# A gated Mamba layer and a ternary feed-forward block on one core: where the statistics of nine tiles are computed, and a new order of the prologue

## The reference, cut to what matters

```python
# x: (4, 512, 512), ctx: (4, 512, 256), all fp32
z   = layernorm(x)                               # (x - mean) / sqrt(var + 1e-5)
u   = silu(conv4(ctx @ in_proj.T) + conv_b)      # (4, 512 channels, 512 steps)
dt_low, Bm, Cm = split(x_proj @ u)               # 16 + 16 + 16 rows
dt  = softplus(dt_low @ dt_proj.T + dt_proj_b)
state = state * exp(dt * A) + (dt * u) * B       # scan over 512 steps, 16 states
y   = (sum_n state * C + D * u) * silu(z)
x1  = x + tanh(g_xattn) * y.T
# feed-forward, rows of 512: three matrices quantised to -1, 0, 1 over mean(|w|)
n   = layernorm(x1);  q = round(127 * rmsnorm(n) / max|rmsnorm(n)|)
h   = silu(q @ w_gate) * (q @ w_up)              # 2048 wide
out = x1 + tanh(g_ffn) * (quantise(rmsnorm(h)) @ w_down)
```

## Time and profile before

| | |
|---|---|
| median of 3 runs | 646.84 us (646.74 to 649.95) |
| the profiled execution's own time | 646.95 us |
| its span, first to last instruction | 644.8 us |
| mean granted TensorE clock | 0.947 |
| start of stage 0, first scan | 75.20 us |
| start of stage 4 | 180.41 us |
| start of stage 15 | 545.01 us |

### The profile page before, as it was taken

The page is one execution under the profiler, slowest core; times in us unless marked ns, Lnnn a source line. Parts: engine busy times, 40 slices in busy tenths (PEclk is TensorE's granted clock), DMA queues, the critical chain, the costliest instruction groups (busy, mean ns, idle before and its releaser), DMA issues. The chain is left out here.

```text
span 644.8 us, 9079 instructions
## 1 busy us (share of the span) xinstructions
PE 505.9 (78%) x2966; PEld 345.2 (54%) x2966; DVE 576.1 (89%) x806; ACT 501.0 (78%) x719; POOL 510.6 (79%) x281
## 2 busy tenths in 40 slices
PE   6998585856757687778767887787787878799997
PEld 2443274745644565556545655565555656564553
DVE  2879999999988999998999999999999999987664
ACT  4889699896976686878688787877786878778784
POOL 2534999999989999999989999999899989931100
PEclk9999869989787889998999899999898999999999
DMA  8993910711830100019301111175111010000001
GB/s 296 400 411 107 376 34 33 262 49 41 338 111 1 33 18 22 13 40 347 115 22 33 34 34 35 33 266 190 34 34 34 33 34 17 1 17 18 16 18 50
DMA packets 29986, 64.47 MB, mean 100 GB/s; under 512 B 3682, under 2 KB 11874, under 8 KB 26867
## 3 DMA queue, kind: packets, MB, share of 16 engines
q1 hardware_dynamic: 29938, 63.89, 27.8%
HBM read 55.75 MB, written 8.13 MB: 99 GB/s over the span
## 5 line engine op out<-in xcount | busy, mean ns | idle before, releaser
L701 POOL TENSOR_TENSOR area_s<-area_s,b_bc 128x1024 f32<-128x1024 f32 x128 | 300.6, 2362 | 22.4 <-DVE u_all L1227 17.7
L428 PE MATMUL pY<-ident,area_s 128*128 128x128 f32 x640 | 107.8, 297 | 83.0 <-DVE area_s L1235 81.8
L428 PEld LDWEIGHTS pY<-ident,area_s 128*128 128x128 f32 x640 | 77.7, 151 | 111.6 <-DVE area_s L1235 76.0
L926 ACT ACTIVATE pA<-dt_all,a_neg 128x512 f32<-128x512 f32 x160 | 107.8, 682 | 23.8 <-DVE area_s L1227 14.5
L1227 DVE TENSOR_TENSOR_SCAN area_s<-pA,area_s 128x512 f32<-128x512 f32 x96 | 114.3, 1204 | 3.7 <-ACT pA L926 3.4
L468 PE MATMUL pG<-wq_gu,area_f 128*128 128x512 fp8e4 x448 | 112.6, 391 | 4.7 <-ACT area_f L878 3.2
L1235 DVE TENSOR_TENSOR area_s<-area_s,pC 128x512 f32<-128x512 f32 x144 | 95.3, 664 | 10.9 <-issue 9.1
L693 POOL TENSOR_TENSOR u_all<-u_all 128x1024 f32<-128x1024 f32 x44 | 103.9, 2361 | 0.0
L422 PE MATMUL pC<-ident,xdT 128*128 128x128 f32 x576 | 94.1, 292 | 1.6 <-DVE xdT L1094 1.3
L422 PEld LDWEIGHTS pC<-ident,xdT 128*128 128x128 f32 x576 | 74.0, 149 | 6.8 <-DVE area_s L1235 4.3
L468 PEld LDWEIGHTS pG<-wq_gu,area_f 128*128 128x128 bf16 x448 | 43.8, 101 | 49.6 <-issue 6.6
(11 more groups left out here) (177 smaller groups left out, 970.4 us busy)
## 6 DMA issues: line engine op xcount, KB each, us to landing
b_bc<-bc_rows SPq DMA_DIRECT2D x16, 1024.0 KB, 7.9
area_s<-x SPq DMA_DIRECT2D x32, 256.0 KB, 2.9
u_all<-bc_rows SPq DMA_DIRECT2D x14, 512.0 KB, 5.7
b_bc<-w_gate SPq DMA_DIRECT2D x1, 4096.0 KB, 14.7
dt_all<-x SPq DMA_DIRECT2D x1, 4096.0 KB, 25.0
area_f<-w_up SPq DMA_DIRECT2D x1, 4096.0 KB, 34.5
area_f<-w_down SPq DMA_DIRECT2D x1, 4096.0 KB, 14.9
out<-area_f SPq DMA_DIRECT2D x16, 256.0 KB, 2.1
```

Source lines behind the costliest of these rows:

```text
L428: mm = pe.matmul(pY[:, k * P:(k + 1) * P], src[:, k * P:(k + 1) * P], ident[:, :], is_transpose=True, start=(first and k == 0), stop=(last ...
L701: gp.tensor_tensor(db[c % NDB], du[s % 2].rearrange("p (a l) -> p a l", a=1).to_broadcast([P, CH, L]), b_bc[:, CH * c:CH * c + CH, :], ALU ...
L926: act.activation(exp_bank(s, n), dt_all[:, s, :], ACT.Exp, scale=a_neg[:, s % NT, n:n + 1]).then_inc(S["s_exp"], 1)
```

## The change

Stages. For the nine tiles t with t % 4 not 0 and t < 12, VectorE's `stats` goes. ScalarE computes the sum of the row (`x_sum`), centres with it (`centre`, now sum - 512 x), and sums the squares (`x_deviation`, followed by a small instruction that writes VE). `xn` has two buffers. In kind B this stands at steps 3 and 4, ahead of `copy_xqT` in ScalarE's order; in kind A at steps 9 and 10, after it. `x_scales` of kind B moves from step 13 to step 11. GpSimd's second `x_rstd` of kind A moves behind `dt_u` and `times_b(s + 1, 0)`. In stages 7, 11 and 15 VectorE does the `residual` instead of GpSimd. On TensorE the last two groups of `hq_transpose` move behind `y_sum(s, 6)` and `c_bcast(s, 7)`.

Prologue. VectorE does the fourth sum of |w_gate| too, GpSimd the four roundings of `w_gate` and, for the last chunk, a clip; VectorE then makes that chunk ternary, behind its statistics of x. Five of the statistics of x come earlier, the last sums are ordered anew, and two waits of ScalarE move from the end of the prologue to its first `z_silu`.

```diff
+def own_stats(t):
+    return t % NT == 0 or t >= UNITS - NT
+def own_residual(s):
+    return s % NT == 2 and s >= NT
+BN_AT = [sum(own_stats(i) for i in range(t)) for t in range(UNITS + 1)]
-        xn = carve(area_f, 4608, D)
+        xn = [carve(area_f, 4608, D), w_xp_sb[:, :, :].rearrange("p k n -> p (k n)")]
...
             def w_total(m):
-                    pe.wait_ge(S["k_abv"], NW - 1 + NW * m)
+                    pe.wait_ge(S["k_abv"], NW + NW * m)
...
             dt_proj(1)
             x_proj(1)
+            w_total(0)
             project(12)
             project(13)
             rows_transpose(1)
-            w_total(0)
...
-                    for r in range(HR):
-                        hq_transpose(t2, r, pG)
+                    hq_transpose(t2, 0, pG)
+                    hq_transpose(t2, 1, pG)
                 y_sum(s, 6)
                 c_bcast(s, 7)
+                if t2 >= 0:
+                    hq_transpose(t2, 2, pG)
+                    hq_transpose(t2, 3, pG)
...
+            def w_round(c):
+                gp.wait_ge(S["k_wm"], 3)
+                gp.tensor_scalar(raw(0, c), raw(0, c), w_inv[:, 0:1], MAGIC, ALU.mult, ALU.add).then_inc(S["k_p1"], 1)
+            def w_clip(c):
+                gp.wait_ge(S["k_p1"], c + 1)
+                gp.tensor_scalar(raw(0, c), raw(0, c), MAGIC + 1.0, MAGIC - 1.0, ALU.min, ALU.max).then_inc(S["k_clip"], 1)
+            conv_sums(0, 10)
+            w_round(0)
+            conv_sums(10, 12)
+            w_round(1)
+            conv_sums(12, 14)
+            w_round(2)
+            conv_sums(14, UNITS)
+            w_round(3)
+            w_clip(3)
...
-            times_b(0, 0)
-            times_b(0, 1)
             gp.wait_ge(S["k_st"], 2 * UNITS)
...
-            times_b(0, 2)
-            times_b(0, 3)
+            for c in range(NDB):
+                times_b(0, c)
...
-                residual(s - 1)
+                if not own_residual(s - 1):
+                    residual(s - 1)
...
             silu(9)
-            act.wait_ge(S["c_g0"], 16)
-            w_abs(0, NW - 1)
             rows_out(1)
+            conv_start(12)
+            conv_start(13)
             silu(10)
             silu(11)
-            conv_start(12)
-            conv_start(13)
-            w_sign(0, 0)
             conv_start(14)
             conv_start(15)
+            w_sign(0, 0)
             rows_out(2)
             silu(12)
             silu(13)
             w_sign(0, 1)
-            w_sign(0, 2)
             silu(14)
             silu(15)
-            w_sign(0, 3)
+            w_sign(0, 2)
...
+            def x_sum(t):
+                act.wait_ge(S["s_x1"], (t // NT) * NT + NT)
+                act.wait_ge(S["f_xn"], t)
+                past(act, S["f_xqp"], t - 1)
+                act.activation(xn[t % 2].rearrange("p (a c) -> p a c", a=NT), tile_x1(t), ACT.Copy, accum_out=col(XSUM)).then_inc(S["f_sum"], 1)
+            def x_deviation(t):
+                act.wait_ge(S["f_xn"], t + 1)
...
+                act.activation(place[:, 0:D], xn[t % 2], ACT.Square, accum_out=col(DEV)).then_inc(S["f_dev"], 1)
+                act.wait_ge(S["f_dev"], t - BN_AT[t] + 1)
+                act.wait_ge(S["f_rr"], t)
+                act.activation(col(VE), col(DEV), ACT.Copy, scale=(1.0 + RMS_EPS) / D, bias=RMS_EPS * LN_EPS * D * D).then_inc(S["f_ve"], 1)
...
                     if n == (2 if t1 % NT else 8):
                         scale_x(t1)
+                    if n == 3 and t1 % NT and (t1 + 1) % NT:
+                        x_sum(t1 + 1)
+                        centre(t1 + 1)
+                    if n == 4 and t1 % NT and (t1 + 1) % NT:
+                        x_deviation(t1 + 1)
                     if n == (4 if t1 % NT else 9):
                         copy_xqT(t1, pG[0][:, :])
...
-                    if n == 10 and (t1 + 1) % NT:
+                    if n == 9 and t1 % NT == 0:
+                        x_sum(t1 + 1)
+                    if n == 10 and t1 % NT == 0:
                         centre(t1 + 1)
+                        x_deviation(t1 + 1)
...
+            def w_ternary(c):
+                dve.wait_ge(S["k_clip"], 1)
+                dve.tensor_scalar(ternary(0, c), raw(0, c), -MAGIC, None, ALU.add, saturate=False).then_inc(S["k_p3"], 1)
...
             w_abs(0, 2)
+            w_abs(0, 3)
+            w_means(0)
             taps(10)
-            w_means(0)
-            w_round(0)
-            w_round(1)
+            for i in range(3):
+                x_stats(i)
             taps(12)
             rows_copy(1)
+            x_stats(3)
+            x_stats(4)
             taps(14)
-            w_round(2)
-            w_round(3)
             rows_copy(2)
-            for i in range(UNITS):
+            for i in range(5, UNITS):
                 x_stats(i)
...
+            w_ternary(3)
             w_abs(1, 0)
...
+                    if n == 3 and own_residual(s - 1):
+                        residual(s - 1)
...
-                    if n == (4 if t1 % NT else 8) and (t1 + 1) % NT:
-                        stats(t1 + 1)
-                    if n == 13 and (t1 + 1) % NT:
+                    if n == (11 if t1 % NT else 13) and (t1 + 1) % NT:
                         x_scales(t1 + 1)
```

More of the change, by code:

```diff
@@ L60 @@
 C_STEP = {2: 3, 3: 4, 6: 7, 7: 11, 10: 12, 11: 13, 14: 15, 15: 16}
-VE, RR, M2, REC1, XS, SS, RH, M3, REC2, FAC, MH = range(11)
+def own_stats(t):
[3 more added lines that the diff above has]
+BN_AT = [sum(own_stats(i) for i in range(t)) for t in range(UNITS + 1)]
+VE, RR, M2, REC1, XS, SS, RH, M3, REC2, FAC, MH, XSUM, DEV = range(13)
 PSS, PMH, SPARE = 20, 24, 28
@@ L368, in rows_transpose @@
                 past(pe, S["k_xdT"], b)
+                past(pe, S["k_wm"], min(b, 1))
                 for t in range(NT):
@@ L461, in xq_transpose @@
                 for k in range(NT):
-                    mm = pe.transpose(bank[:, k * P:(k + 1) * P], xn[:, k * P:(k + 1) * P], ident[:, :])
+                    mm = pe.transpose(bank[:, k * P:(k + 1) * P], xn[t % 2][:, k * P:(k + 1) * P], ident[:, :])
                 mm.then_inc(S["f_xqp"], 1)
@@ L661, in _, with conv_sums @@
             gp.wait_ge(S["k_const"], 9)
-            for i in range(UNITS):
-                gp.wait_ge(S["k_tap"], i + 1)
-                gp.wait_ge(S["k_acc"], 2 * i + 2)
-                gp.tensor_tensor(xc[i % 4][:, 1:L], xc[i % 4][:, 1:L], xb[i % 4][:, 1:L], ALU.add).then_inc(S["k_conv"], 1)
+            def conv_sums(first, last):
+                for i in range(first, last):
+                    gp.wait_ge(S["k_tap"], i + 1)
+                    gp.wait_ge(S["k_acc"], 2 * i + 2)
+                    gp.tensor_tensor(xc[i % 4][:, 1:L], xc[i % 4][:, 1:L], xb[i % 4][:, 1:L], ALU.add).then_inc(S["k_conv"], 1)
+            def w_round(c):
[13 more added lines that the diff above has]
+            w_clip(3)
             def residual(s):
@@ L673, in x_rstd @@
             def x_rstd(t):
[L674 removed]
+                gp.wait_ge(S["f_ve"], t + 1)
                 past(gp, S["f_xs"], 5 * t)
@@ L747, in _ @@
                 times_c(s, 1)
-                if t1 % NT == 0:
-                    x_rstd(t1 + 1)
                 times_b(s, NDB + 3)
@@ L753, in _ @@
                     times_b(s + 1, 0)
+                if t1 % NT == 0:
+                    x_rstd(t1 + 1)
                 times_c(s, 2)
@@ L863, in centre @@
             def centre(t):
-                act.wait_ge(S["f_bn"], 3 * t + 2)
-                past(act, S["f_xqp"], t)
-                act.activation(xn.rearrange("p (a c) -> p a c", a=NT), tile_x1(t), ACT.Identity, scale=-1.0, bias=mv[:, 0:1]).then_inc(S["f_xn"], 1)
+                past(act, S["f_xqp"], t - 1)
+                out = xn[t % 2].rearrange("p (a c) -> p a c", a=NT)
+                if own_stats(t):
+                    act.wait_ge(S["f_bn"], 2 * BN_AT[t] + 2)
+                    act.activation(out, tile_x1(t), ACT.Identity, scale=-1.0, bias=mv[:, 0:1]).then_inc(S["f_xn"], 1)
+                else:
+                    act.wait_ge(S["f_sum"], t - BN_AT[t] + 1)
+                    act.activation(out, tile_x1(t), ACT.Identity, scale=-float(D), bias=col(XSUM)).then_inc(S["f_xn"], 1)
+            def x_sum(t):
+                act.wait_ge(S["s_x1"], (t // NT) * NT + NT)
+                act.wait_ge(S["f_xn"], t)
+                past(act, S["f_xqp"], t - 1)
+                act.activation(xn[t % 2].rearrange("p (a c) -> p a c", a=NT), tile_x1(t), ACT.Copy, accum_out=col(XSUM)).then_inc(S["f_sum"], 1)
+            def x_deviation(t):
+                act.wait_ge(S["f_xn"], t + 1)
+                if (t - 1) % NT:
+                    place = squares_out(t)
+                    past(act, S["f_sq"], 2 * t - 3)
+                else:
+                    place = squares_out(t - 1)
+                    past(act, S["f_dn"], t - 2)
+                act.activation(place[:, 0:D], xn[t % 2], ACT.Square, accum_out=col(DEV)).then_inc(S["f_dev"], 1)
```

(11 more changed lines are left out.)

25 lines of the change are left out of this document (10 added, 15 removed).

## The result

The changed kernel takes 651.69 us (median of 20 runs, 649.82 to 652.55), the kernel before 648.59 us beside it (20 runs, 645.47 to 652.54): ratio 1.0052, 95% interval 1.0037 to 1.0066. My 647.0 was wrong, the time lies 0.2 us above the range, and my chance for "slower" was 0.17. Of the 4.7 us between 647.0 and 651.69, 3.1 are the change, which I had put at 0.2; the rest is the kernel before itself, which measures 1.75 us more in 20 runs than in the three that I started from (646.84). The profiled execution has a span of 649.4 us against 644.8, granted clock 0.942 against 0.947.

A forecast was written before the change was run, and what follows sets the result against it. The prediction took ScalarE's chain around the gate's silu to bound the later half of a stage as much as VectorE. Stages + 1.6 and prologue - 1.4 on 646.95 gave 647.15 us, range 639.5 to 651.5.

The forecast's parts named there:

- kind B: Stages 5, 6, 9, 10, 13, 14: 2.8 us won, 2 x 0.1 at full clock plus 4 x 0.65 at low clock.
- kind A: Stages 4, 8, 12: ScalarE's statistics delay the first silu; 8 and 12 lose 1.45 us each, 4 nothing; 2.9 us lost.
- prologue: Work ahead of the stages: 1.4 us won; bounds 4.0 won and nothing won.
- the residual's price: Stages 7, 11, 15: VectorE's residual costs 0.66 us like another VectorE product, 0.6 less overlap, replacing 1.27 on GpSimd.
- Kind C: Stages 7, 11, 15: residual ahead of h_max and later transposes of h lose 0.5 us each, 1.5 us; upper bound 3 x 1.2.
- the rounding's row: Prologue: VectorE's ternary chunk priced from the trace's rounding at 1.3 to 2.3 us, 1.8 used.
- ScalarE's new work: Per tile, nine times: sum and sum of squares at 0.8 us each plus a small instruction of 0.3, 1.9 us.
- the 0.65 us for each low-clock stage: Stages 5, 9, 13, 14: x_scales lies in the product's wait for TensorE, so 0.65 us won each, between nothing and 1.0.
- ScalarE's standstill: In kind B, ScalarE's wait before copy_xqT, up to 4.1 us, holds the 2.5 us of statistics work at no cost.
- The wait for the store: Prologue: z_silu(1) needs the last store_bc, landing at 81.2 us, so it goes 1.4 us earlier, not 4.
- the third rival: Prologue: GpSimd rounds at its two-input rate, 4.7 us, making z_silu(1) 9.3 us late; 658 us, chance 0.09.
- The first rival: Whole kernel: VectorE is the bound after all, its saved time is kept; 8.0 us won, 639, half 643; chance 0.30.

The follow-up runs named there:

- experiment 2: Changed kernel with TensorE's old order of the transposes of h, residuals still on VectorE: 649.34 us, 1.0017 of the kernel before.
- experiment 5: Kernel before with only the residuals of stages 7, 11 and 15 moved to VectorE at step 3: 652.97 us, 1.0054 of the kernel before.
- experiment 4: Changed kernel with VectorE's residual one step later, where GpSimd is idle: 645.77 us, 0.9955 of the kernel before.
- experiment 1: Changed kernel with the three residuals back on GpSimd, nothing else: 644.27 us, 0.9932 of the kernel before.
- experiment 6: Against experiment 1: statistics of tile t1 + 1 in stages 4, 8 and 12 back on VectorE; 641.66 us, 0.9863 of the kernel before.
- experiment 9: Kernel before with only the new prologue, its stages untouched: 646.19 us, 0.9964 of the kernel before.
- experiment 7: Against experiment 1: x_scales of kind B back at step 13 instead of 11; 636.96 us, 0.9797 of the kernel before.
- experiment 8: Against experiment 1: the prologue's last store_bc issued ahead of three loads in the DMA queue; 644.38 us, 0.9903 of the kernel before.
- the best version: Changed kernel with the edits of experiment 1, experiment 6, experiment 7 and experiment 8 together: 633.97 us, 0.9748 of the kernel before.

## Why the prediction was wrong

**The step that failed is the residual's price.** "Three residuals come, at the 0.66 us of the like product on VectorE" took `gated_y` of the earlier trace rows as the like product. It has the engine, shape and type, but it reads pY from PSUM; the residual reads szT and area_s from SBUF, while GpSimd is busy 31.22 of 31.30 us in stage 11, nearly all of it with products of two SBUF tensors. The true price there was 1.73 to 2.56 us (experiments 2 and 5 and the kernel after), 0.68 where GpSimd was idle (experiment 4). Kind C: +1.5 predicted, +5.8 measured, and undoing it wins 7.4 us, more than the whole 4.7 by which the forecast was off. The bound I gave (3 x 1.2) did not hold it either: it was made of rows of other instructions, none of which met that condition. The trace before could have raised the doubt. It has no row of the residual's kind beside a busy GpSimd, but it shows the two engines holding each other up, in the four roundings of the earlier trace rows:

```profile
43.53 2.47 DVE L1115 TENSOR_SCALAR b_bc<-b_bc,w_inv 128x2048 f32<-128x2048 f32 x2
51.37 4.06 DVE L1115 TENSOR_SCALAR b_bc<-b_bc,w_inv 128x2048 f32<-128x2048 f32 x2
```

```profile
48.05 2.50 POOL L666 TENSOR_TENSOR area_s<-area_s 128x511 f32<-128x511 f32 x2 [7.35 <-DVE area_s L1076]
50.88 3.48 POOL L666 TENSOR_TENSOR area_s<-area_s 128x511 f32<-128x511 f32 x2 [0.32 <-DVE area_s L1076]
```

Two roundings take 2.47 us while GpSimd is idle (1278 ns each in the mean), and the other two 4.06 (2071 ns each) beside GpSimd's convolution sums, which take 3.48 instead of 2.50. The mean of all four, 1675 ns, hid it, and my "by the rounding's row 1.3 to 2.3 us" had the spread but did not ask what made it.

The Trainium skill has this rule (SBUF — State Buffer, Who interferes with whom): a VectorE instruction with two SBUF inputs contends with a GpSimd instruction that reads SBUF, through a shared read interface, and the interface is locked, so that whichever starts second is blocked until the first is through. The trace agrees, nine times of nine: an end 0.54 or 0.55 us behind GpSimd's, and 0.45 us more for GpSimd's next. I weighed two other rules of the skill and not this one, which spoke against the change.

**Kind A: mechanism right, size not.** Stages 8 and 12 were to lose 1.45 each. At full clock it is 1.07 (experiments 1 and 6). The term mis-sized is ScalarE's new work, 1.9 us: from the start of `copy_xqT` to the first silu it was 4.23 us before and is 5.30 in experiment 1, so with the 0.42 us of idle time filled the work is 1.49, because neighbours overlap more than I allowed (the sum takes 0.62 of ScalarE's time and not 0.8, the squares with the small instruction 0.86 and not 1.1). That explains 2.1 of the 4.9 us by which the two stages grew. The other 2.7 go with a low clock: stage 8 after has 0.82, the lowest of the four windows above. Experiment 9 shows the same stages 1.3 and 1.7 us longer than before, at 0.90 and 0.91, without this edit in them. Whether the change itself draws the low clock there was not shown. ScalarE became what is waited for, as said: in experiment 1, at full clock, the fifteenth scan of stage 8 stands behind the exponential:

```profile
339.33 1.22 DVE L1299 TENSOR_TENSOR_SCAN area_s<-pA,area_s 128x512 f32<-128x512 f32 x1 [0.79 <-ACT pA L986]
```

Stage 4 was to stay as it was and is 0.8 shorter (35.00 to 34.17), but so it is in experiments 9 (34.14) and 5 (34.04), so this is neither by the statistics nor by the prologue.

**Kind B: right at full clock, in part luck in the sum.** -2.8 predicted, -2.4 measured; the undisturbed stage was to be 32.2 and is 32.22 in four of six. But the 0.65 us for each low-clock stage, most of the term, is not confirmed: stages 5 and 9, still at a low clock, won 0.14 and 0.37, and the rest came from stages 13 and 14 (0.75 and 1.06), which ran at full clock this time. ScalarE's standstill did hold the statistics; it still waits in front of `copy_xqT`, 23.7 us in nine stages where it was 37.2 in ten:

```profile
ACT area_f L938 <- PE pG L477: 23.7, 9, 4.1
```

Experiment 7 confirms why so little came of it: x_scales in front of the product took 0.91 us back in each stage at full clock.

**The prologue: right in its chain, half its size.** The ternary chunk was ready 1.6 us earlier than I had it (60.4 against 62.0): 0.6 by its duration (1.20 against 1.8), and 1.0 because the new order fills 2.5 us of VectorE's waits (66.25 - 6.7 + 2.2 = 61.75, it started at 59.23) where I allowed 1.5. The wait for the store was there, but 2.2 us, and experiment 8 shows that taking it away moved the start of stage 4 by 0.3 us at most, within the spread. GpSimd's rounding at 1.97 us settles the third rival, which does not occur. The first rival, VectorE as the bound after all, fell in kind A and, with experiment 7, is half true of kind B: without x_scales in the way, the microsecond taken from VectorE there came off the stage (32.28 to 31.31). No run separates this from the other half of the move, `centre` leaving ScalarE's full half (0.6 us).

**With the residual at its true price** (a stage 2.0 longer, as stages 11 and 15 of experiment 2, and 0.35 for the order behind it), kind C gives 3 x 2.35 = +7.1 instead of +1.5, and with the prologue's -2.9 the prediction's sum is 646.95 + 7.1 - 2.8 + 2.9 - 2.9 = 651.2; the profiled execution took 651.18, the median is 651.7. That it comes so close is luck in part: kind C measured +5.8, since stage 7 of the kernel before was already long at a low clock (32.62), and kind A +4.1, and the two misses cancel.

## What to carry to other kernels

Before pricing an elementwise instruction by a like one, compare where each operand lies as well as shape and type: here a VectorE addition with both inputs in SBUF, started beside GpSimd's two-input product, lasted until that product was through. So before moving such an operation from GpSimd to VectorE, look whether GpSimd is idle at that place, or one input is in PSUM. The time does not show as waiting: it lies inside the instruction's own duration, so compare the longest and the shortest of one kind, and not the mean alone. And when a move buys little, look what it was put in front of: five small instructions two steps later were worth 5.4 us in the six B stages here, more than the 2.4 that kind B won with its statistics on ScalarE and these instructions in front.

## What the runs showed of the hardware

- VectorE, 128x512 fp32, both inputs in SBUF: 0.68 us with GpSimd idle; beside GpSimd's two-input product it ends 0.54 to 0.55 us behind that product (1.73 to 2.56 us in all), and GpSimd's next takes 2.79 to 2.82 instead of 2.36.
- With one operand in PSUM the same engine does the same shape in 0.66 us beside the same GpSimd product (L1307 at 418.98, 0.27 us into L732's 2.36), and a maximum over one SBUF tensor of 128x2048 is not held up beside the next product either (2.27 us, L1262 at 421.54; 2.28 in the mean before).
- One SBUF tensor can be enough: VectorE's fp32 rounding of 128x2048 takes 1.28 us with GpSimd idle and 2.07 in the mean beside GpSimd's sums (kernel before). The other way round, GpSimd's small tensor_scalar (128x16) takes 1.07 us, started 0.25 us behind VectorE's ternary chunk (59.23, 1.20 us), where it took 0.27 before.
- GpSimd's one-input work on 128x2048 fp32: 1.97 us with a tensor's scalar and a constant, 1.89 with two constants, 0.92 to 0.96 ns an element; its two-input product takes 2.3 ns an element.
- The kernel before spreads over 645.5 to 652.5 us in the 20 runs beside the kernel after, the best version over 633.7 to 634.7 in six. With the same work in the stages, single stages with low-clock stretches were 0.7 to 1.7 us longer (experiment 9).
